# A graph layer on one core: TensorE waits for the end of its own rank products and of its own second filter layer

## The chip, the cores and the metric

The kernel runs on one NeuronCore of a Trainium2 chip. The engines named here are TensorE (PE, matmuls; its weight loads are listed apart as PEld), VectorE (DVE), ScalarE (ACT), GpSimd (POOL) and SyncE (SP, which issues DMAs). Each runs its own stream of instructions in order, and they meet only through semaphores. The metric is the device time of one execution in microseconds (us), the median of several runs; smaller is better.

## The reference, cut to what matters

A continuous-filter graph layer over 12,500 nodes with 128 features and 400,000 edges, sorted by `dst`:

```python
h = relu(layernorm(x)) @ W_in2f.T                    # 12500 x 128
Wij = smu(edge_attr @ W_f1.T + b_f1) @ W_f2.T + b_f2 # 400000 x 128, "two filter layers"
Wij = Wij * edge_weight[:, None]
x_ij = h[dst] * Wij
agg = segment_sum(x_ij, src)                         # sum of the edges of each node
out = x + smu(agg @ W_o1.T + b_o1) @ W_o2.T + b_o2
```

`smu(x)` is a smooth activation made here of a Gelu and a linear part. The edges come sorted by `dst`, but are summed by `src`, so the kernel has to sort the messages itself.

## The kernel before, in words

**Units.** The edges (padded) are cut into 784 units of 512 edges (4 tiles of 128). Each engine runs its own version of the function `step(st)` once for each beat, a beat being one unit; `st.at(k)`, `st.has(k)`, `st.items(k)` speak of the unit that lies k beats back, so each step works on several units at once, as a software pipeline. TensorE's step does, in this order:

- `filter1(n)` (L1202): first filter layer, into PSUM bank `p_z`. ScalarE takes the Gelu (`gelu`, L707), VectorE adds the linear part (`act`, L979).
- `bucket_sum(it)` (L1256, `p_seg`): for messages sorted in an earlier round, products of rows `seg` with one-hot matrices `seg_hot`. VectorE builds the one-hots (L1029) and adds the result to `agg` (L1042).
- `turn(n-2)` (L1213): transposes the product `hg` of unit n-2 into `p_m`, from where ScalarE writes the weighted messages `msg` (L723). It waits for VectorE's product (`s_prod`).
- `rank(n-1)` (L1228, L1244): eight small products into `p_pos` that count, for each edge, how many edges of its bucket came before it. The last one raises `s_rank`; VectorE's `places` (L1003) waits for that and works out the row of each edge, `row_numbers` (L1014).
- `targets(n-1)` (L1222): gathers `h[dst]` as a product with a window of rows (`win`), into `p_h`; ScalarE copies it to `hg` (L717).
- `filter2(n-1)` (L1207): second filter layer into `p_w`, raises `s_w`; VectorE multiplies it into `hg` (L995), which is what the next beat's `turn` waits for.

**GpSimd.** For each unit it waits for the row numbers, the messages and for `filter2` of two units later (`s_w`), and then issues four indirect DMAs, one for each tile, that scatter the messages into `sorted_rows` in DRAM (L588):

```python
wait_for(pool, s_idx, n, 1, 1)
wait_for(pool, s_msg, n, 1, 1)
wait_for(pool, s_w, n, 1, 3)
for k in range(tiles):
    pool.indirect_dma_start(out=sorted_rows[:, :], ...)
```

Messages, row numbers and one-hots have rings of four buffers (`RING`), so VectorE and ScalarE wait for the scatter of four units ago.

**Rounds.** The units form ten rounds of 112, 112, 112, 112, 80, 80, 56, 40, 40 and 40 units. The messages of a round fall into 112 buckets. Those of round r are summed (`bucket_sum`) during the beats of round r+1, eight beats late, spread evenly; round 9 is summed behind the last unit. A bucket takes 5, 5, 5, 5, 4, 4, 3, 2, 2, 2 tiles in rounds 0 to 9; of those with 4 and 3 tiles two buckets go together in one item, of those with 2 tiles four do. Each tile costs TensorE two matmul instructions. Parts of rounds 0 to 3 are hardware loops of four beats, all else is straight code.

The order of each engine's work is the order in which `step` is written. Nothing else schedules it. `wait_for(eng, sem, at, times, plus)` makes an engine wait until a semaphore holds the unit's number plus an offset.

Of the kernel before, what the change touches and what calls it, by code (L numbers as in the profile page):

```python
# [77 lines left out]
def wait_for(eng, sem, at, times=1, plus=0):  # L78
    v = at.value(times, plus)
    if at.i is None and v <= 0:  # L80
        return
    eng.wait_ge(sem, v)


def build(nc, n_nodes, n_edges, n_real, F, R, t):
# [47 lines left out]
    with ctx:  # L133
# [6 lines left out]
        def sem(name):  # L140
            return ctx.enter_context(nc.semaphore(name))
# [68 lines left out]
        with ExitStack() as ahead_only:  # L210
# [67 lines left out]
        s_z, s_gelu, s_smu, s_w, s_pick, s_ph, s_hg, s_prod, s_turn, s_msg, s_key = (  # L278
            sem(n) for n in ("s_z", "s_gelu", "s_smu", "s_w", "s_pick", "s_ph", "s_hg", "s_prod", "s_turn", "s_msg", "s_key"))
        s_hot, s_rank, s_place, s_idx, s_total, s_count = (  # L280
            sem(n) for n in ("s_hot", "s_rank", "s_place", "s_idx", "s_total", "s_count"))
# [34 lines left out]
        def h_at(st, lag):  # L316

            at = st.c - H_FROM - lag
            if st.i is not None or st.rnd > 0 or at < 0 or at % 2:
                return None  # L320
            g = H_AHEAD + at // 2
            return g if g < n_h else None
# [850 lines left out]
        def _(pe):  # L1173
            pe.wait_ge(s_pool, 4)

            def transpose_nodes(g):
                pe.wait_ge(s_hn, g + 1)
                if g >= 1:
                    pe.wait_ge(s_hTs, g)
                for k in range(H_TILES):  # L1180
                    last = pe.transpose(p_seg[0][:, k * LANES:(k + 1) * LANES], hn[:, g % 2, k, :], ident[:, :])
                last.then_inc(s_hT, 1)

            def first_layer(g):
                pe.wait_ge(s_hTs, g + 1)
                if g >= 1:
                    pe.wait_ge(s_hr, g)
                for k in range(H_TILES):
                    last = pe.matmul(h_bank(g)[:, k, :], hT[:, g % 2, k, :], w_in[:, :], start=True, stop=True)
                last.then_inc(s_hm, 1)  # L1190
# [7 lines left out]
            def filter1(n, p, q, v):  # L1198
                if v == 0:
                    wait_for(pe, s_attr[q], p.over(2), 16, 16)  # L1200
                wait_for(pe, s_smu, n)
                pe.matmul(p_z[:, :], w_f1[:, :], attr[:, q, v * UNIT:(v + 1) * UNIT], start=True, stop=True).then_inc(s_z, 1)  # L1202

            def filter2(n, v):
                wait_for(pe, s_smu, n, 1, 1)
                wait_for(pe, s_prod, n)
                pe.matmul(p_w[:, :, :].rearrange("f k e -> f (k e)"), w_f2[:, :], act1[:, v, :], start=True, stop=True).then_inc(s_w, 1)  # L1207

            def turn(n, v):
                wait_for(pe, s_prod, n, 1, 1)  # L1210
                wait_for(pe, s_msg, n)
                for k in range(TILES_U):
                    last = pe.transpose(p_m[:, k, :], hg[:, v, k, :], ident[:, :])  # L1213
                last.then_inc(s_turn, 1)

            def targets(n, p, q, v):
                if v == 0:
                    wait_for(pe, s_win[q], p.over(2), 16, 16)
                wait_for(pe, s_pick, n, 1, 1)
                wait_for(pe, s_hg, n)  # L1220
                for part in range(PARTS):
                    last = pe.matmul(p_h[:, :, :].rearrange("f k e -> f (k e)"), win[:, q, part * F:(part + 1) * F], pick[:, v, :],  # L1222
                                     start=(part == 0), stop=(part == PARTS - 1))
                last.then_inc(s_ph, 1)

            def counted(slot, rnd):
                for k in range(TILES_U):
                    last = pe.matmul(p_pos[:, 0:BUCKETS], not_before[:, :], onehot[:, slot, k, :], start=False, stop=False,  # L1228
                                     skip_group_check=True)
                return last  # L1230

            def rank(n, slot, rnd, opens):
                wait_for(pe, s_hot, n, 1, 1)
                wait_for(pe, s_place, n)
                if opens:
                    if rnd > 0:
                        counted((slot - 1) % RING, rnd - 1).then_inc(s_total, 1)
                        pe.wait_ge(s_count, rnd)
                    pe.matmul(p_pos[:, 0:BUCKETS], step_rows[:, :], seeds[:, rnd % BUFS, :], start=True, stop=False,
                              skip_group_check=True)  # L1240
                else:
                    counted((slot - 1) % RING, rnd)
                for k in range(TILES_U):
                    last = pe.matmul(p_pos[:, 0:BUCKETS], before[:, :], onehot[:, slot, k, :], start=False, stop=False,  # L1244
                                     skip_group_check=True)
                last.then_inc(s_rank, 1)

            def bucket_sum(it):
                wait_for(pe, s_segld[it.slot], it.x.over(SEGS), 16, 16)
                wait_for(pe, s_seghot, it.x, 1, 1)  # L1250
                if it.opens:
                    wait_for(pe, s_agg, it.n, 1, -1)
                for l in range(it.some):
                    out = p_seg[it.bank][:, it.col + l * NODE_P:it.col + (l + 1) * NODE_P]
                    for k in range(it.tiles):
                        last = pe.matmul(out, seg[:, it.slot, l * it.tiles + k, 0:F], seg_hot[:, it.slot, l * it.tiles + k, :],  # L1256
                                         start=(k == 0), stop=(k == it.tiles - 1))
                last.then_inc(s_seg, 1)

            def hidden(g, turn):  # L1260
                b, n = g % 2, turn * n_groups + g
                if turn == 0:
                    pe.wait_ge(s_agg, first_sum[rounds - 1] + g + 1)
                if n > 1:
                    pe.wait_ge(s_oe, n - 1)
                pe.matmul(p_u[b][:, :, :].rearrange("p a n -> p (a n)")[:, 0:GROUP], w_o1[:, :],
                          agg[:, g * NODE_G:(g + 1) * NODE_G, :], start=True, stop=True).then_inc(s_u, 1)
# [11 lines left out]
            def step(st):  # L1279
                if st.rnd == 0 and st.i is None and st.c == 1:  # L1280
                    pe.wait_ge(s_scaled, 1)
                    filter2(st.at(1), st.v(1))
                    pe.wait_ge(s_pool2, 2)
                    pe.wait_ge(s_seeds, 1)
                    rank(st.at(1), st.ring(1), st.rnd_of(1), st.opens(1))
                    targets(st.at(1), st.pair(1), st.q(1), st.v(1))
                    filter1(st.at(), st.pair(), st.q(), st.v())
                    transpose_nodes(1)
                    return
                if st.rnd == rounds - 1 and st.c == 0:  # L1290
                    pe.wait_ge(s_ld, 16 * N_LD)
                    pe.wait_ge(s_scaled_out, 1)
                if st.has():
                    filter1(st.at(), st.pair(), st.q(), st.v())
                for it in st.items(1):
                    bucket_sum(it)
                if st.has(2):
                    turn(st.at(2), st.v(2))
                if st.has(1):
                    rank(st.at(1), st.ring(1), st.rnd_of(1), st.opens(1))  # L1300
                    targets(st.at(1), st.pair(1), st.q(1), st.v(1))
                    filter2(st.at(1), st.v(1))
                if st.rnd == 0 and st.i is None and st.c == 2:
                    first_layer(1)
                if h_at(st, 1) is not None:
                    transpose_nodes(h_at(st, 1))
                if h_at(st, 3) is not None:
                    first_layer(h_at(st, 3))
                if st.i is None and st.rnd == rounds and st.c == 1:
                    pe.wait_ge(s_place, n_units)  # L1310
                    counted((n_units - 1) % RING, rounds - 1).then_inc(s_total, 1)
                if st.group(2) is not None:
                    hidden(st.group(2), 0)
                if st.group(4) is not None:
                    last_layer(st.group(4), 0)

            beats(pe, step)

            def everywhere():
# [84 lines left out]
```

## Time and profile before

| | |
|---|---|
| median of 3 runs | 4146.94 us (4142.5 to 4153.49) |
| the profiled execution, first to last instruction | 5246.4 us; no other time is reported for it |
| its mean granted TensorE clock | 0.902 of full speed |
| busy in it: PE, DVE, ACT, POOL | 4105.5, 3459.8, 2190.0, 3044.9 us |
| TensorE idle ahead of `turn` (L1213) in it | 905.9 us |

The profiled execution took 1,099 us longer than the median of the runs without a profile. So its sums of idle time can't be read as those of an ordinary run; durations of single instructions and the distance between two that follow each other without a wait can. The ends of TensorE's matmuls are modelled, and consecutive ones overlap in the records; the distance between two starts tells what one costs in a stream.

### The profile page before, as it was taken

The page shows a single profiled execution, that of the slowest core. Times are in us where ns is not written, and L with a number is a line of the kernel's source. Part 1 is how long each engine was busy: PE and PEld are TensorE (multiplying, and loading weights), DVE is VectorE, ACT ScalarE, POOL GpSimd, SP SyncE. Part 2 cuts the span into 40 slices and gives each one's busy share as a digit, 9 for nine tenths or more (in the row PEclk, how much of TensorE's full clock was granted, in tenths as well). Part 3 has the DMA queues.
Part 4 walks back from the last instruction along what each step waited for, and adds up shares of the span by engine and source line. Part 5 has one row for each costly group of instructions (what it writes and reads, how often), then busy time and mean ns, then how long its engine had stood idle before and what let it go on. Part 6 is the DMA issues. An engine that isn't in the chain of part 4 may idle for free.

```text
span 5246.4 us, 97364 instructions
## 1 busy us (share of the span) xinstructions
PE 4105.5 (78%) x23774; PEld 2777.5 (53%) x23774; DVE 3459.8 (66%) x11848; ACT 2190.0 (42%) x7302; POOL 3044.9 (58%) x3173
## 2 busy tenths in 40 slices
PE   6677667777777777777777778788888888887888
PEld 3344335555555555555555555555555666655557
DVE  6666556666666666666666666666666777766677
ACT  4566444444443344444443434434443443334333
POOL 4666655555555555555555555655555555555553
PEclk8888889988988989989889899998888999998999
DMA  6455445554444444444444445554444555554446
GB/s 181 122 147 147 126 118 144 147 144 146 146 133 125 125 124 125 131 127 125 127 126 121 134 145 148 148 153 132 132 133 136 158 157 152 159 160 136 139 137 206
DMA packets 459545, 737.14 MB, mean 141 GB/s; under 512 B 87168, under 2 KB 255466, under 8 KB 459104
## 3 DMA queue, kind: packets, MB, share of 16 engines
q1 hardware_dynamic: 291606, 461.44, 33.5%
q0 software_dynamic: 100000, 206.60, 11.7%
q10 hardware_dynamic: 67626, 65.48, 3.8%
q8 instruction: 129, 2.11, 0.2%
q14 instruction: 184, 1.51, 0.1%
HBM read 465.36 MB, written 267.82 MB: 140 GB/s over the span
## 4 chain that ended last, share of the span: by engine, by line
PE 36%; another core or an unknown queue 25%; DVE 16%; issue 14%; ACT 7%; ACTq 1%; DMA 1%; DVEq 1%; SPq 0%; POOL 0%
PE p_w L1207 7%; PE p_h L1222 7%; PE p_seg L1256 6%; PE p_m L1213 6%; PE p_z L1202 5%; DVE product L1003 4%; DVE hg L995 4%; ACT msg L723 3%; PE p_pos L1244 2%; DVE onehot L988 2%; PE p_pos L1228 2%; DVE act L979 2%; ACT hg L717 2%; DVE pick L983 1%
## 5 line engine op out<-in xcount | busy, mean ns | idle before, releaser
L588 POOL DMA_INDIRECT sorted_rows<-msg,row_idx x3125 | 3004.5, 961 | 2122.6 <-issue 904.5
L1003 DVE CUSTOM_DVE_ANT_0 product<-onehot,p_pos,start_at 128x112 bf16<-128x112 bf16 x3136 | 849.2, 326 | 1096.3 <-remote 1012.3
L723 ACT ACTIVATE msg<-p_m,weight 128x128 f32<-128x128 f32 x3136 | 893.5, 369 | 1439.1 <-remote 786.2
L1256 PEld LDWEIGHTS p_seg<-seg_hot,seg 128*128 128x128 f32 x8288 | 1066.4, 196 | 464.5 <-issue 461.8
L1213 PE MATMUL p_m<-ident,hg 128*128 128x128 f32 x3136 | 561.2, 307 | 905.9 <-DVE hg L995 649.7
L1256 PE MATMUL p_seg<-seg_hot,seg 128*128 128x112 f32 x8288 | 1085.6, 279 | 117.3 <-issue 107.8
L1213 PEld LDWEIGHTS p_m<-ident,hg 128*128 128x128 f32 x3136 | 384.5, 155 | 1102.0 <-DVE hg L995 675.3
L1207 PE MATMUL p_w<-act,w_f 128*128 128x512 f32 x1568 | 932.0, 679 | 10.4 <-issue 5.7
L1202 PE MATMUL p_z<-attr,w_f 128*128 128x512 f32 x1568 | 853.8, 626 | 56.3 <-issue 24.3
L995 DVE SCALAR_TENSOR_TENSOR hg<-p_w,bias_w,hg 128x512 f32<-128x512 f32 x784 | 588.0, 750 | 464.9 <-remote 155.4
L717 ACT COPY hg<-p_h 128x512 f32<-128x512 f32 x784 | 461.9, 589 | 878.4 <-remote 592.3
L1222 PE MATMUL p_h<-pick,win 128*128 128x512 bf16 x2352 | 767.9, 442 | 7.2 <-issue 5.1
L707 ACT ACTIVATE gelu<-p_z 128x512 f32<-128x512 f32 x784 | 468.5, 598 | 579.5 <-PE p_z L1202 324.7
L979 DVE SCALAR_TENSOR_TENSOR act<-p_z,gelu 128x512 f32<-128x512 f32 x784 | 537.1, 685 | 138.8 <-issue 93.9
L1202 PEld LDWEIGHTS p_z<-attr,w_f 128*128 128x128 f32 x1568 | 325.4, 212 | 510.9 <-issue 465.5
L1029 DVE SCALAR_TENSOR_TENSOR seg_hot<-seg,p_iota 128x560 f32<-128x560 f32 (+2 forms) x700 | 582.0, 837 | 11.9 <-DMA seg<-sorted_rows 7.3
L988 DVE TENSOR_TENSOR onehot<-p_iota,node_l 128x448 bf16<-128x448 f32 x784 | 481.7, 614 | 0.0
L1207 PEld LDWEIGHTS p_w<-act,w_f 128*128 128x128 f32 x1568 | 355.1, 227 | 170.6 <-issue 67.7
L1244 PE MATMUL p_pos<-onehot,before 128*128 128x112 bf16 x3136 | 320.1, 232 | 0.0
L1228 PE MATMUL p_pos<-onehot,not_before 128*128 128x112 bf16 x3136 | 316.1, 230 | 0.0
L983 DVE TENSOR_SCALAR pick<-ends,win_row 128x512 bf16<-128x512 uint16 x784 | 289.4, 369 | 0.0
L1222 PEld LDWEIGHTS p_h<-pick,win 128*128 128x128 bf16 x2352 | 218.9, 110 | 129.0 <-issue 56.4
(114 smaller groups left out, 2157.8 us busy)
## 6 DMA issues: line engine op xcount, KB each, us to landing
seg<-sorted_rows SPq DMA_DIRECT2D x448, 322.5 KB
seg<-sorted_rows SPq DMA_DIRECT2D x196, 516.0 KB
ends<-ends SPq DMA_DIRECT2D x392, 256.0 KB
sorted_rows<-msg,row_idx POOLq DMA_INDIRECT x3125
sorted_rows<-zero_rows ACTq DMA_DIRECT2D x336, 129.0 KB
win<-h SPq DMA_DIRECT2D x392, 96.0 KB
attr<-in_attrT SPq DMA_DIRECT2D x392, 80.0 KB
seg<-sorted_rows SPq DMA_DIRECT2D x56, 387.0 KB
```

Source lines behind the costliest of these rows:

```text
L588: pool.indirect_dma_start(out=sorted_rows[:, :], out_offset=bass.IndirectOffsetOnAxis(ap=row_idx[:, slot, k:k + 1], axis=0), in_=msg[:, sl ...
L723: last = act.activation(msg[:, slot, k, 0:F], p_m[:, k, :], ACT.Copy, scale=weight[:, bass.ds(n.value(TILES_U, k), 1)])
L979: dve.scalar_tensor_tensor(act1[:, v, :], p_z[:, :], SMU_L, gelu[:, v, :], ALU.mult, ALU.add).then_inc(s_smu, 1)
L988: dve.tensor_tensor(onehot[:, slot, :, :], p_iota[:, 0:BUCKETS].unsqueeze(1).to_broadcast([LANES, TILES_U, BUCKETS]), node_l[:, bass.ds(n. ...
L995: dve.scalar_tensor_tensor(hg[:, v, :, :], p_w[:, :, :], bias_w[:, :], hg[:, v, :, :], ALU.add, ALU.mult).then_inc(s_prod, 1)
L1003: last = dve.tensor_tensor_reduce(out=product[:, k, :], in0=onehot[:, slot, k, :], in1=p_pos[:, 0:BUCKETS], scale=1.0, scalar=start_at[:, ...
L1029: dve.scalar_tensor_tensor(seg_hot[:, it.slot, 0:n, :], seg[:, it.slot, 0:n, F:F + 1].to_broadcast([LANES, n, NODE_P]), -float(LANES * (it ...
L1202: pe.matmul(p_z[:, :], w_f1[:, :], attr[:, q, v * UNIT:(v + 1) * UNIT], start=True, stop=True).then_inc(s_z, 1)
L1207: pe.matmul(p_w[:, :, :].rearrange("f k e -> f (k e)"), w_f2[:, :], act1[:, v, :], start=True, stop=True).then_inc(s_w, 1)
L1213: last = pe.transpose(p_m[:, k, :], hg[:, v, k, :], ident[:, :])
L1222: last = pe.matmul(p_h[:, :, :].rearrange("f k e -> f (k e)"), win[:, q, part * F:(part + 1) * F], pick[:, v, :], start=(part == 0), stop= ...
L1256: last = pe.matmul(out, seg[:, it.slot, l * it.tiles + k, 0:F], seg_hot[:, it.slot, l * it.tiles + k, :], start=(k == 0), stop=(k == it.ti ...
```

## The change

TensorE's step gets two waits. The first stands between `rank` and `targets` and asks for the `s_rank` that its own last rank product has just been told to raise. The second stands behind `filter2` and asks for the `s_w` that this same layer raises. Nothing is removed or moved.

```diff
                 if st.has(1):
                     rank(st.at(1), st.ring(1), st.rnd_of(1), st.opens(1))
+                    wait_for(pe, s_rank, st.at(1), 1, 1)
                     targets(st.at(1), st.pair(1), st.q(1), st.v(1))
                     filter2(st.at(1), st.v(1))
+                    wait_for(pe, s_w, st.at(1), 1, 1)
```

The very first beat with such work is written out apart and has no new wait; 783 of the 784 units get both.

Where the waits land is to be seen in the order of TensorE's instructions, with the semaphores that each one waits for. First a beat in the middle of the loop body in round 1. Before, from the rank products to the bucket sum of the next beat:

```order
L1228 MATMUL p_pos<-onehot,not_before 128x112 [waits s_place,s_hot]
L1228 MATMUL p_pos<-onehot,not_before 128x112 x3
L1244 MATMUL p_pos<-onehot,before 128x112 x4
L1222 MATMUL p_h<-pick,win 128x512 [waits s_hg,s_pick]
L1222 MATMUL p_h<-pick,win 128x512 x2
L1207 MATMUL p_w<-act,w_f 128x512 [waits s_prod,s_smu]
L1202 MATMUL p_z<-attr,w_f 128x512 [waits s_smu]
```

The same beat of the changed kernel:

```order
L1228 MATMUL p_pos<-onehot,not_before 128x112 [waits s_place,s_hot]
L1228 MATMUL p_pos<-onehot,not_before 128x112 x3
L1244 MATMUL p_pos<-onehot,before 128x112 x4
L1222 MATMUL p_h<-pick,win 128x512 [waits s_hg,s_pick,s_rank]
L1222 MATMUL p_h<-pick,win 128x512 x2
L1207 MATMUL p_w<-act,w_f 128x512 [waits s_prod,s_smu]
L1202 MATMUL p_z<-attr,w_f 128x512 [waits s_smu,s_w]
```

The first target product now waits for the rank products, and the next beat's first filter layer (`p_z`) for the second filter layer (`p_w`). No row has changed its place.

At the end of a loop body the row behind `filter2` is no matmul. Before, TensorE's rows around the loop's counter (L401) in a straight piece ahead of the loop's next part:

```order
L1222 MATMUL p_h<-pick,win 128x512 x2
L1207 MATMUL p_w<-act,w_f 128x512 [waits s_prod,s_smu]
L401 REGISTER_ALU
L401 COMPARE_AND_BRANCH
L1202 MATMUL p_z<-attr,w_f 128x512 [waits s_smu,s_attr0]
```

And of the changed kernel:

```order
L1222 MATMUL p_h<-pick,win 128x512 x2
L1207 MATMUL p_w<-act,w_f 128x512 [waits s_prod,s_smu]
L401 REGISTER_ALU [waits s_w]
L401 COMPARE_AND_BRANCH
L1202 MATMUL p_z<-attr,w_f 128x512 [waits s_smu,s_attr0]
```

Here the second wait holds the counting and the branch themselves, once in four units of a loop.

## Rows read from the trace of the kernel before

**Rows 1.** The page's first line: the span.

```profile
span 5246.4 us, 97364 instructions
```

**Rows 2.** Waits by engine and line: total us, times, longest us.

```profile
DVE product L1003 <- remote: 1012.3, 310, 6.3
...
PE p_m L1213 <- DVE hg L995: 649.7, 302, 7.0
```

**Rows 3.** Timeline, 2000 to 2030 us: start, duration, engine, line, count, idle before.

```profile
2006.61 0.36 PE L1244 MATMUL p_pos<-onehot,before 128*128 128x112 bf16 x4
...
2013.07 0.33 DVE L1003 CUSTOM_DVE_ANT_0 product<-onehot,p_pos,start_at 128x112 bf16<-128x112 bf16 x1 [3.06 <-remote]
```

**Rows 4.** Timeline of POOL: the first scatter and the last two.

```profile
39.03 1.12 POOL L588 DMA_INDIRECT sorted_rows<-msg,row_idx  x1 [33.06 <-issue]
...
5130.91 0.95 POOL L588 DMA_INDIRECT sorted_rows<-msg,row_idx  x1 [0.30 <-issue]
5132.17 0.96 POOL L588 DMA_INDIRECT sorted_rows<-msg,row_idx  x1 [0.30 <-issue]
```

**Rows 5.** Groups by line and form: the scatters, and VectorE's one-hots for the sums.

```profile
L588 POOL DMA_INDIRECT sorted_rows<-msg,row_idx x3125 | 3004.5, 961 | 2122.6 <-issue 904.5 <-remote 706.2 <-PE p_w L1207 362.4
...
L1029 DVE SCALAR_TENSOR_TENSOR seg_hot<-seg,p_iota 128x560 f32<-128x560 f32 x448 | 324.7, 731 | 3.9 <-DMA ends<-ends 3.9
...
L1029 DVE SCALAR_TENSOR_TENSOR seg_hot<-seg,p_iota 128x896 f32<-128x896 f32 x196 | 211.3, 1078 | 7.4 <-DMA seg<-sorted_rows 7.3
...
L1029 DVE SCALAR_TENSOR_TENSOR seg_hot<-seg,p_iota 128x672 f32<-128x672 f32 x56 | 46.0, 845 | 0.6 <-DMA ends<-ends 0.6
```

**Rows 6.** Timeline of PE: one whole beat in round 2 without stops.

```profile
2001.60 0.66 PE L1213 MATMUL p_m<-ident,hg 128*128 128x128 f32 x4 [1.49 <-DVE hg L995]
2002.09 0.36 PE L1228 MATMUL p_pos<-onehot,not_before 128*128 128x112 bf16 x4
2002.29 0.36 PE L1244 MATMUL p_pos<-onehot,before 128*128 128x112 bf16 x4
2002.48 0.81 PE L1222 MATMUL p_h<-pick,win 128*128 128x512 bf16 x3
2003.13 1.02 PE L1207 MATMUL p_w<-act,w_f 128*128 128x512 f32 x2
2003.99 1.02 PE L1202 MATMUL p_z<-attr,w_f 128*128 128x512 f32 x2
2004.85 1.26 PE L1256 MATMUL p_seg<-seg_hot,seg 128*128 128x112 f32 x10
2005.95 0.63 PE L1213 MATMUL p_m<-ident,hg 128*128 128x128 f32 x4
2006.41 0.36 PE L1228 MATMUL p_pos<-onehot,not_before 128*128 128x112 bf16 x4
```

**Rows 7.** Timeline of PE: a sum of 16 matmuls and what follows it.

```profile
3600.11 1.93 PE L1256 MATMUL p_seg<-seg_hot,seg 128*128 128x112 f32 x16
3601.88 0.60 PE L1213 MATMUL p_m<-ident,hg 128*128 128x128 f32 x4
```

**Rows 8.** Source view of L1244, 2100 to 2137 us: shortest, median and longest ns.

```profile
L1244 PE MATMUL p_pos<-onehot,before x24: 212/213/213, 2100.6 to 2132.3; 128*128 128x112 bf16 x24
```

**Rows 9.** Timeline, 2000 to 2030 us: what PE waited for, and who waited for PE.

```profile
2000.79 0.75 DVE L995 SCALAR_TENSOR_TENSOR hg<-p_w,bias_w,hg 128x512 f32<-128x512 f32 x1 [1.66 <-remote]
...
2002.39 1.14 ACT L723 ACTIVATE msg<-p_m,weight 128x128 f32<-128x128 f32 x4 [0.94 <-PE p_m L1213]
```

**Rows 10.** Timeline of PE behind a long stop.

```profile
2017.02 1.49 PE L1222 MATMUL p_h<-pick,win 128*128 128x512 bf16 x3
2018.30 1.53 PE L1207 MATMUL p_w<-act,w_f 128*128 128x512 f32 x2
```

**Rows 11.** Windows: busy PE, PEld, DVE, ACT, POOL with counts, PE clock, DMA share.

```profile
500.00:1000.00 500.00, 348.57 (x1803) 210.78 (x1802) 299.13 (x1076) 213.40 (x705) 298.35 (x309) 0.88 0.48 133
...
3000.00:3500.00 500.00, 407.71 (x2540) 288.28 (x2539) 343.93 (x1169) 201.06 (x692) 294.41 (x307) 0.94 0.51 149
```

## The prediction

> **What bounds the kernel now.** I read the page first. Its span is 5246.4 us [rows 1], 1,099 us above the median of the runs, 4146.94 us. So before anything is summed it has to be said what the profiled execution has that the others lack.
>
> The list of waits says it. VectorE's `product` waited 310 times for something unnamed, 1012.3 us in all, and TensorE's `turn` 649.7 us for the product that VectorE then made late [rows 2]. The timeline shows one such case: the rank products were over at 2006.61 + 0.36 = 2006.97, and VectorE, which waits for nothing else there, started at 2013.07 [rows 3], 6.1 us later. News of TensorE's finished work arrives late in this execution, and 1012 us of it is about the excess of 1,099 us. I take that lag for a thing of the recorded execution; that it is none of the others' follows only from the size of the excess.
>
> What then bounds an ordinary run? GpSimd's timeline: two scatters without a wait between them start 1.26 us apart (0.96 busy, 0.30 issue), the first at 39.03 us, the last ends at 5133.1 us [rows 4]. There are 3125 [rows 5]. Back to back they take 3125 x 1.26 = 3938 us; with 39 us ahead of them and 5246.4 - 5133.1 = 113 us behind, 4090 us. The median is 57 us above. So an ordinary run is one chain of scatters on GpSimd, nearly without holes: **5.04 us a unit**.
>
> TensorE's beat comes from the timeline where it doesn't stop [rows 6], always from start to start: `turn` 0.46 (0.49 behind a wait), rank 0.20 + 0.19, `targets` 0.65, `filter2` 0.86, `filter1` 0.86, ten sum matmuls 1.10. That is 3.25 us without sums plus 0.11 us for each sum matmul (sixteen take 1.77 us [rows 7]). How many there are in a unit follows from the rounds; the one-hots' rows confirm the total: 448 items of 5 tiles, 196 of 8, 56 of 6 [rows 5], 4144 tiles or 8288 matmuls.
>
> - 120 units ahead of the first sums: 3.25 us a beat
> - 336 units (rounds 1 to 3), 10 matmuls each: 4.35
> - 80 (round 4), 14: 4.79
> - 80 (round 5) and 40 (round 8), 11.2: 4.48
> - 56 (round 6), 16: 5.01
> - 40 (round 7), 16.8: 5.10
> - 32 (round 9), 14: 4.79
>
> TensorE has 0.7 us to spare in most beats at full clock, and nothing in rounds 6 and 7.
>
> **The change part by part.** Nothing is removed or moved; 783 units get two waits. Each wait holds TensorE until its own last matmul is out and the semaphore is back.
>
> What one costs isn't in this trace, since TensorE never waits there for itself. It is made of three parts. First the drain: a lone rank product takes 213 ns [rows 8] though in the stream they start 50 ns apart, and the row of four ends at 2002.65 while `targets` has started at 2002.48; 0.17 us. For `filter2` the row ends at 2004.15, the next starts at 2003.99; 0.16 us [rows 6]. Second the handover: the nearest row is TensorE resuming 0.06 us after VectorE's end (2001.54 to 2001.60); the other way, ScalarE starts 0.13 us after TensorE's modelled end (2002.26 to 2002.39) [rows 6, 9]. Third the weight load, which no longer hides under the matmul before it: the resumed `turn` takes 0.49 us and the unstopped one 0.46 [rows 6], 0.03 us. I take 0.17 + 0.06 + 0.03, about 0.25 us a wait, **0.5 us a unit**, since the waiter is TensorE as in the 0.06 row. Bounds: the drain alone, 0.33 us a unit; with the long handover, 0.68. Neither end can be a gain by itself, as a wait only holds. Far beyond these ends lies the 6.1 us of rows 3: it would make the profiled execution much longer, but it isn't what the ordinary runs show.
>
> The Trainium skill, "Advanced Engine Details and Errata", section Network/Comms, has a sequencer read a semaphore's value in 50 to 100 ns. By that figure as the handover, without the weight load, the sum below would be 59 to 80 us (an estimate from that page), and no row here shows the reading by itself.
>
> What is queued behind the waits: behind the first `targets` and `filter2`, which ScalarE's `hg`, VectorE's product and, through `s_w`, GpSimd wait for; behind the second `filter1`, the sums and the next `turn`. Does that lateness reach VectorE first? Counting from the start of `turn`, `filter2` is over at 2.39 + 0.16 us, with the first wait 2.8. VectorE is busy 3459.8 us in 784 units, 4.4 us a unit; all of that but the product itself, 0.75 us [rows 9], comes ahead of its need for `filter2`, about 3.6 us. So the first wait is hidden from VectorE by 0.8 us of its own work; if that cover were gone, 0.25 us a unit or 196 us would show. What counts is TensorE's beat against GpSimd's 5.04 us.
>
> With 0.5 us more a beat:
>
> - first 120 units 3.75, rounds 1 to 3 4.85, rounds 5 and 8 4.98: all still below 5.04, no cost. The idle time ahead of `turn` pays for it.
> - round 4: 5.29, 0.25 over, x 80 = 20 us
> - round 6: 5.51, 0.47 x 56 = 26 us
> - round 7: 5.60 instead of 5.10, 0.50 x 40 = 20 us
> - round 9: 5.29, 0.25 x 32 = 8 us
>
> Sum 74 us: **4147 + 74 = 4221 us**, 1.8% slower. With 0.33 us a unit the same list gives 6 + 17 + 13 + 3 = 39 us (4186). With 0.68, round 4 gives 34, rounds 5 and 8 now 0.12 x 120 = 14, then 36, 27 and 14: 125 us (4272). The loop's branch, now held by the second wait too, comes once in four units of rounds 0 to 3, where 0.19 us of a beat are still free; I cost it at nothing. If it took over 0.8 us, it would show.
>
> These sums are made on the median, with durations of the profiled execution; by its own span the forecast says nothing, since its lag may shrink or grow with the waits.
>
> **The rivals.**
>
> *The idle time swallows it.* TensorE has 906 us of idle time ahead of `turn` in the profile, 650 of them a wait for VectorE [rows 2]. If a self-wait costs 0.1 us, or if the dense rounds have slack that my averages miss (the row of four scatter buffers carries a slow beat over a fast one), only rounds 6 and 7 show it: at 0.2 us a unit 10 + 8 = 18 us, at 0.1 us a unit 7 us. Against it: the drain alone is 0.33 us. Time 4147 to 4159, say 4152. Chance 0.20.
>
> *The clock falls.* Behind the long stop TensorE ran `targets` in 1.28 us from start to start instead of 0.65 [rows 6, 10]: exactly half, 1.2 GHz instead of 2.4 GHz. The granted clock was 0.88 in an early window with 349 us of busy TensorE and 0.94 in one with 408 [rows 11]. If the small holes made 5% of TensorE's work run at the lower level, each beat would be 0.05 x 4.35 = 0.22 us longer, 0.72 in all, and the list gives 150 us (4297); at 10%, 0.93 in all, 288 us (4435), as rounds 1 to 3 then pass 5.04 too. Against it: the holes take the place of a longer one ahead of `turn`, so TensorE is idle no more than before. The Trainium skill, "TensorE: Matmul & The Clock Gate", section "A second HAM failure mode: psum-queue depth-cycling", reports just this, frequent micro-idles between groups of matmuls making the clock swing; the long stops of this trace show the fall, its short ones don't. Chance 0.10.
>
> *Faster.* If part of the lag of rows 3 is there in ordinary runs too, because TensorE races ahead of its own news, a TensorE held back would hand `s_rank` and `s_w` over sooner and GpSimd would have fewer holes. It can win no more than the 57 us above the bare chain: 4090 us. It decides once it wins back more than the waits cost, 39 us or more by the sums above; half of 57 isn't enough. Chance 0.07.
>
> **How the numbers follow.** The main case (4186 to 4272, 4221 the likeliest) has 0.63, the rivals 0.20, 0.10 and 0.07. A difference under 0.3% (12 us) can't be told from none. Slower: 0.63 + 0.10 = 0.73; same: 0.20; faster: 0.07. The range goes from 4142, which takes in the idle-time case, to 4300, which takes in the main case and the mild end of the clock case; what is left out is the faster case and most of the clock case, 0.07 + 0.07, and a few parts in a hundred between.
>
> **What would show it.** In the profile after: `targets` starting some 0.3 us after the last rank product's start instead of 0.05 us, and `filter1` likewise 0.25 us later behind `filter2`; TensorE's idle time ahead of L1222 and L1202 now tenths of a us in each of 783 units, that ahead of `turn` smaller; scatters still 1.26 us apart. Wrong would make it: an own wait that takes far more than 0.3 us; a mean clock below 0.88; beats of rounds 1 to 3 above 5.04 us; or scatters that are less than 1.26 us apart in ordinary runs, as then rounds 1 to 3 pay too, up to 0.5 x 336 = 168 us.

## The result and the profile after

The changed kernel takes 4244.39 us (median of 4 runs, 4236.25 to 4246.63), the kernel before 4148.44 us beside it: a ratio of 1.0228, 95% interval 1.0215 to 1.0241. That is 96 us or 2.3% slower, where 74 us or 1.8% (4221 us) was forecast. The last comparison below (e9 to e12) stands apart, because on its chip the unchanged kernel took 5249 us, as in the recorded execution shown above, instead of 4149 us.

The page of the changed kernel, with the lines that answer to [rows 1] and the table of before:

```profile
span 4233.8 us, 98063 instructions
...
PE 3901.1 (92%) x23774; PEld 2470.1 (58%) x23774; DVE 3461.2 (82%) x11848; ACT 2246.9 (53%) x7302; POOL 3043.5 (72%) x3173
```

The run that this is the record of took 4236.25 us, 2.5 us more than its span. The three others took 4244 to 4247 us, so the record is of the fastest run, 8 us below the median; its mean granted clock is 0.992. It has no lag, and idle times too can be read here as those of an ordinary run.

TensorE's timeline in round 5, the answer to [rows 6]: one beat with both waits and a sum of 16 matmuls (the last row opens the next beat).

```profile
3001.61 0.60 PE L1213 MATMUL p_m<-ident,hg 128*128 128x128 f32 x4
3002.05 0.36 PE L1228 MATMUL p_pos<-onehot,not_before 128*128 128x112 bf16 x4
3002.25 0.36 PE L1244 MATMUL p_pos<-onehot,before 128*128 128x112 bf16 x4
3002.67 0.82 PE L1222 MATMUL p_h<-pick,win 128*128 128x512 bf16 x3
3003.32 1.02 PE L1207 MATMUL p_w<-act,w_f 128*128 128x512 f32 x2
3004.41 1.12 PE L1202 MATMUL p_z<-attr,w_f 128*128 128x512 f32 x2
3005.37 1.94 PE L1256 MATMUL p_seg<-seg_hot,seg 128*128 128x112 f32 x16
3007.14 0.60 PE L1213 MATMUL p_m<-ident,hg 128*128 128x128 f32 x4
```

Read the starts. From the last rank row to the targets it is now 0.42 us instead of 0.19: the first wait costs 0.23 us. From `filter2` to `filter1` it is 1.09 us instead of 0.86, again 0.23. And `filter1` itself now takes 0.96 us to the next start instead of 0.86: 0.10 us that the prediction had no term for. The beat is 5.53 us; without waits the prediction's rows give 3.25 + 16 x 0.11 = 5.01. The 3.25 has `turn` at its 0.49 us behind a wait. Where nothing stops, `turn` takes 0.44 us, and most such beats without the new waits are 4.96 or 4.97 us long (the record of e3 below, round 6), so the pair of waits adds 0.56.

At the end of a loop body the second wait costs more. The same view at about 1500 us, in round 2:

```profile
1503.47 1.02 PE L1207 MATMUL p_w<-act,w_f 128*128 128x512 f32 x2
1505.09 1.12 PE L1202 MATMUL p_z<-attr,w_f 128*128 128x512 f32 x2 [0.60 <-PE p_w L1207]
1506.05 1.26 PE L1256 MATMUL p_seg<-seg_hot,seg 128*128 128x112 f32 x10
1507.15 0.60 PE L1213 MATMUL p_m<-ident,hg 128*128 128x128 f32 x4
```

1.62 us from start to start instead of 0.86, once in four beats.

The waits of the changed kernel (total us, times, longest us), beside which stand those of [rows 2]:

```profile
PEld p_z L1202 <- PE p_w L1207: 379.1, 420, 1.7
...
PEld p_h L1222 <- PE p_pos L1244: 164.2, 748, 0.3
...
PE p_m L1213 <- DVE hg L995: 121.4, 94, 3.4
```

TensorE now waits for itself some 750 times at the targets, 0.22 us each. The 379.1 us of the first row are no price: a stop of PEld is counted from the end of its last weight load, and that load hides under the matmul ahead (at 3004.40 it counts 0.89 us where the start of the matmul moved by 0.23), so most of it is time in which `filter2` still ran. For VectorE's product TensorE waits 121 us. In the record of e5 below, whose time is that of before, that is 295.6 us, and its idle time ahead of `turn` from all causes is 433.9 us, against 123.7 us here: the new waits took the place of part of the old one.

GpSimd over 500 us of rounds 1 and 2, and over 500 us that take in the end of round 5, round 6 and the start of round 7, the answer to [rows 11] (columns as there):

```profile
1000.00:1500.00 500.00, 469.15 (x2872) 296.98 (x2871) 413.68 (x1454) 272.95 (x892) 379.40 (x396) 1.00 0.62 172
...
3000.00:3500.00 500.00, 480.78 (x3044) 317.04 (x3043) 415.24 (x1360) 249.31 (x830) 353.53 (x370) 1.00 0.62 176
```

396 scatters in 500 us are one in 1.263 us: GpSimd has no hole here, and it has none in the record of e5 either (395). From 3000 us on there are 370, where e5's record has 389, and TensorE is busy 480.8 of 500 us. That is the kink that the prediction was built on: GpSimd is the bound in rounds 1 to 3, TensorE in the dense ones.

### The profile page after: what moved, and what is told of

It is laid out like the page before. It is cut to its first block, busy times and chain, and to the rows that moved or that the text cites. A ratio compares the mean times of both kernels' runs of the same rounds, so it can differ in the third digit from the quotient of the medians.

```text
span 4233.8 us, 98063 instructions
## 1 busy us (share of the span) xinstructions
PE 3901.1 (92%) x23774; PEld 2470.1 (58%) x23774; DVE 3461.2 (82%) x11848; ACT 2246.9 (53%) x7302; POOL 3043.5 (72%) x3173
## 4 chain that ended last, share of the span: by engine, by line
PE 64%; POOL 12%; issue 11%; DMA 6%; DVE 4%; ACT 2%; ACTq 1%; SPq 0%; POOLq 0%; DVEq 0%
PE p_seg L1256 16%; PE p_z L1202 13%; POOL sorted_rows L588 12%; PE p_w L1207 11%; PE p_h L1222 11%; PE p_m L1213 6%; DMA sorted_rows<-msg,row_idx 5%; PE p_pos L1244 3%; PE p_pos L1228 2%; DVE hg L995 1%; DVE product L1003 1%; DVE seg_hot L1029 1%; ACT msg L723 1%; PE p_seg L1189 1%; DVE act L979 1%
## 5 line engine op out<-in xcount | busy, mean ns | idle before, releaser
L1256 PEld LDWEIGHTS p_seg<-seg_hot,seg 128*128 128x128 f32 x8288 | 1029.0, 192 | 307.4 <-issue 304.6
L1256 PE MATMUL p_seg<-seg_hot,seg 128*128 128x112 f32 x8288 | 1024.8, 275 | 8.3 <-issue 8.3
L1207 PE MATMUL p_w<-act,w_f 128*128 128x512 f32 x1568 | 811.7, 600 | 4.2 <-DVE act L979 4.2
L1222 PE MATMUL p_h<-pick,win 128*128 128x512 bf16 x2352 | 652.5, 387 | 50.1 <-DMA win<-h 1.7
L1202 PEld LDWEIGHTS p_z<-attr,w_f 128*128 128x128 f32 x1568 | 234.5, 189 | 747.6 <-PE p_w L1207 379.1
L1213 PE MATMUL p_m<-ident,hg 128*128 128x128 f32 x3136 | 479.4, 276 | 123.7 <-DVE hg L995 121.4
L1207 PEld LDWEIGHTS p_w<-act,w_f 128*128 128x128 f32 x1568 | 302.5, 193 | 120.9 <-issue 9.2
L1014 DVE TENSOR_TENSOR row_idx<-place,place_max 128x4 int32<-128x4 f32 x784 | 126.0, 161 | 266.3 <-DMA sorted_rows<-msg,row_idx 257.7
L1222 PEld LDWEIGHTS p_h<-pick,win 128*128 128x128 bf16 x2352 | 166.6, 98 | 269.7 <-PE p_pos L1244 164.2
L1244 PE MATMUL p_pos<-onehot,before 128*128 128x112 bf16 x3136 | 284.2, 214 | 0.0
```

## The experiments

Each ratio is to the kernel before, run beside it. A unit is 1/784 of the work.

**e1, the first wait only.**

```diff
                     rank(st.at(1), st.ring(1), st.rnd_of(1), st.opens(1))
+                    wait_for(pe, s_rank, st.at(1), 1, 1)
                     targets(st.at(1), st.pair(1), st.q(1), st.v(1))
```

> Only the wait behind the rank products. My theory: a beat of TensorE costs time only above the 5.04 us that GpSimd's four scatters take, and this wait is 0.23 us (the distance from the last row of rank products to the target products grew from 0.19 to 0.42 us in the profile of the changed kernel). Round 6 is then 5.24 us a beat (0.20 x 56 = 11 us), round 7 5.33 instead of 5.10 (0.23 x 40 = 9 us), all others below 5.04: 20 us slower, about 4168 us, far less than half of the 96 us. Rival, every wait costs the same wherever it stands (0.06 us each of 1566): half of 96, 48 us slower, 4196 us.

Measured: 4187.45 us against 4149.48, ratio 1.009 (1.0073 to 1.0107), 38 us. Nearer to the rival's 48 than to my 20.

**e2, the second wait only.**

```diff
                     filter2(st.at(1), st.v(1))
+                    wait_for(pe, s_w, st.at(1), 1, 1)
```

> Only the wait behind the second filter layer. My theory: it costs 0.33 us a beat in straight code (0.23 more ahead of the first filter layer, 0.10 more in it), so rounds 4, 6, 7 and 9 pay 6 + 17 + 13 + 3 = 39 us: about 4187 us; in the loops of rounds 1 to 3 it costs 0.46 on the mean, which 4.35 us a beat still hides. The two waits alone then give 20 + 39 = 59 us, less than the 96 us together. Rival, every wait costs the same wherever it stands: 48 us each, and the two alone add up to the 96 us.

Measured: 4190.09 us, ratio 1.0099 (1.0082 to 1.0116), 41 us, the number that my theory had, but in part by luck. Round by round (the lengths come below) its record has 14 us in round 0, where the theory had nothing, and 6 us in round 6, where it had 17; rounds 4 and 7 cost 5 and 16 us against 6 and 13. The two waits alone make 79 us; together they make 96. So they don't simply add up, though less sharply than 59 against 96.

**e3 and e4, both waits, but only in the beats of rounds 0 to 3, or only in those of rounds 4 to 9.**

```diff
+                    if st.rnd < 4:
+                        wait_for(pe, s_rank, st.at(1), 1, 1)
                     targets(st.at(1), st.pair(1), st.q(1), st.v(1))
                     filter2(st.at(1), st.v(1))
+                    if st.rnd < 4:
+                        wait_for(pe, s_w, st.at(1), 1, 1)
```

(e4 has `st.rnd >= 4` in both places.)

> Both waits, but only in the beats of rounds 0 to 3 (448 of 784 units). My theory: GpSimd's chain hides them there, at most the loops' beats (4.35 + 0.56 + 0.13 = 5.04 us) touch the bound: 0 to 18 us slower, 4148 to 4166 us. Rival, the same cost in every unit: 448/784 of 96 us, 55 us slower.

> Both waits, but only in the beats of rounds 4 to 9 (336 of 784 units). My theory: nearly the whole loss is made here: with 0.56 us a beat, round 4 pays 0.31 x 80 = 25 us, round 6 0.53 x 56 = 30, round 7 0.56 x 40 = 22, round 9 0.31 x 32 = 10, rounds 5 and 8 nothing: 87 us slower, 4235 us. Rival, the same cost in every unit: 336/784 of 96 us, 41 us slower.

Measured: e3 4170.1 us, 1.0049 (1.003 to 1.0068), 21 us for 448 units; e4 4232.59 us, 1.0208 (1.0191 to 1.0225), 83 us for 336 units. The rival's 55 and 41 us are both out. e3 is above the 4148 to 4166 us that I had allowed, and not for the reason given there: the loops' beats cost nothing (rounds 1 to 3 of its record take 1701.3 us, those of e4 without waits 1705.1), while its round 0 took 606.7 us against 582.9. The pair of waits costs 0.05 us a unit over rounds 0 to 3 and 0.25 us over rounds 4 to 9.

These two also give a baseline round by round: what e4 does in rounds 0 to 3, and e3 in rounds 4 to 9, is the kernel before. Each round opens with one product of `seeds` (L1239), and the source view gives the start of the first and the last in a stretch. The changed kernel:

```profile
L1239 PE MATMUL p_pos<-seeds,step_rows x2: 224/263/302, 21.5 to 622.3; 128*128 128x112 bf16 x2
L1239 PE MATMUL p_pos<-seeds,step_rows x2: 222/223/224, 2323.1 to 2749.3; 128*128 128x112 bf16 x2
L1239 PE MATMUL p_pos<-seeds,step_rows x2: 223/248/273, 3162.9 to 3471.8; 128*128 128x112 bf16 x2
L1239 PE MATMUL p_pos<-seeds,step_rows x2: 222/223/224, 3700.8 to 3910.3; 128*128 128x112 bf16 x2
```

e4 for the early rounds:

```profile
L1239 PE MATMUL p_pos<-seeds,step_rows x2: 223/262/301, 21.2 to 604.1; 128*128 128x112 bf16 x2
L1239 PE MATMUL p_pos<-seeds,step_rows x2: 223/223/223, 2309.2 to 2736.7; 128*128 128x112 bf16 x2
```

e3 for the late ones, and its span:

```profile
span 4169.4 us, 97350 instructions
...
L1239 PE MATMUL p_pos<-seeds,step_rows x2: 223/224/224, 2329.5 to 2736.1; 128*128 128x112 bf16 x2
L1239 PE MATMUL p_pos<-seeds,step_rows x2: 223/224/225, 3146.2 to 3439.4; 128*128 128x112 bf16 x2
L1239 PE MATMUL p_pos<-seeds,step_rows x2: 223/224/224, 3646.6 to 3851.8; 128*128 128x112 bf16 x2
```

The lengths are the differences of these starts:

| beats of | without waits, us | with, us | more | forecast |
|---|---|---|---|---|
| round 0 (112) | 582.9 | 600.8 | +18 | 0 |
| rounds 1 to 3 (336) | 1705.1 | 1700.8 | -4 | 0 |
| round 4 (80) | 406.6 | 426.2 | +20 | 20 |
| round 5 (80) | 410.1 | 413.6 | +4 | 0 |
| round 6 (56) | 293.2 | 308.9 | +16 | 26 |
| round 7 (40) | 207.2 | 229.0 | +22 | 20 |
| round 8 (40) | 205.2 | 209.5 | +4 | 0 |
| round 9 and what follows | 317.6 | 323.5 | +6 | 8 |

The left column with 21.2 us ahead of it sums to 4149 us, within the spans of the kernel before beside these runs (4142 to 4151 us): the pieces fit. But each length is from one record. That of e5 below, whose time is also that of before, has 592.4 us for round 0 and lies within 4 us of the left column everywhere else. So a round's cost is known to some 4 us, and that of round 0 only as 8 to 18 us.

**Where round 0 lost its time.** GpSimd in windows of 60 us (busy with count, PE clock, DMA share, GB/s), the changed kernel first, then e4, which has no waits here:

```profile
240.00:300.00 60.00, 41.35 (x44) 0.97 0.63 172
300.00:360.00 60.00, 40.72 (x43) 0.94 0.62 168
360.00:420.00 60.00, 40.73 (x43) 0.94 0.61 162
```

```profile
240.00:300.00 60.00, 45.31 (x48) 0.97 0.69 182
300.00:360.00 60.00, 44.21 (x46) 1.00 0.66 182
360.00:420.00 60.00, 45.66 (x48) 1.00 0.72 190
```

130 scatters instead of 142: twelve times 1.26 us is 15 us. (e5's record has 136 in these windows.) In these beats TensorE, ScalarE and VectorE also make the node layer's rows (`transpose_nodes`, `first_layer`). I had counted the beats of round 0 as 3.25 us throughout and forgotten that work. That it is this work that takes up the slack is read from the place, not tried by a kernel of its own; e10 and e11 below show only that a longer GpSimd covers the waits here too.

**e5, the same two waits, each one group of matmuls later.**

```diff
                 if st.has():
                     filter1(st.at(), st.pair(), st.q(), st.v())
+                if st.has(2):
+                    wait_for(pe, s_w, st.at(2), 1, 1)
...
                     targets(st.at(1), st.pair(1), st.q(1), st.v(1))
+                    wait_for(pe, s_rank, st.at(1), 1, 1)
                     filter2(st.at(1), st.v(1))
```

> The same two semaphores are waited for, each one group of matmuls later: the rank products' behind the target products (0.65 us of other work in between), the second filter layer's behind the next beat's first filter layer (0.86 us in between). My theory: what costs is the array running dry, not the wait as an instruction; here the semaphore has long risen when TensorE asks, so the time is that of before, 4149 us, within 10 us. Rival, the wait itself costs (sequencer time, or its instructions): the 96 us of both waits, 4245 us.

Measured: 4151.88 us against 4153.08, ratio 0.9994 (0.9984 to 1.0003). As many waits, no cost, and that in the dense rounds as well, where nothing would hide one: rounds 4, 6 and 7 take 406.2, 290.8 and 207.0 us, against the 406.6, 293.2 and 207.2 of the table. So it isn't the instruction or the sequencer's work on it that costs, but TensorE standing still until its own last matmul is out and the semaphore is back. One group of other matmuls in between is enough. How the price divides into drain, handover and weight load this run doesn't tell.

**e6, a third wait of the same kind.**

```diff
                     turn(st.at(2), st.v(2))
+                    wait_for(pe, s_turn, st.at(2), 1, 1)
```

> A third wait of the same kind, for TensorE's own turned product right behind turn. It makes a beat 0.23 to 0.25 us longer again: 0.8 us in straight code, 0.9 to 1.0 in the loops. My theory: rounds 1 to 3 now stand above GpSimd's 5.04 us too, so this wait costs far more than the two before it together would suggest: 0.25 x 300 in the loops, 0.24 x 120 in rounds 5 and 8, 0.25 x 208 in rounds 4, 6, 7 and 9, about 75 + 29 + 52 = 156 us on top of the 96: about 4400 us. Rival, the same price for each wait: 48 us more, 4293 us.

Measured: 4385.76 us, ratio 1.0558 (1.054 to 1.0576): all three cost 233 us, so the third adds 137 us to the 96 of the first two. Expected were 156 us, by the rival 48. The openings in its record show that rounds 1 to 3 pay now:

```profile
L1239 PE MATMUL p_pos<-seeds,step_rows x2: 223/262/301, 21.2 to 631.2; 128*128 128x112 bf16 x2
L1239 PE MATMUL p_pos<-seeds,step_rows x2: 222/222/223, 2403.2 to 2848.0; 128*128 128x112 bf16 x2
```

2403.2 - 631.2 = 1772 us for 336 units, 5.27 us each, against 1705 us without waits and 1701 with two. With two waits the loops' beats stood at 5.05 us on the mean; the third wait is the one that lifts TensorE over GpSimd's 5.04 us.

**e7 and e8, the first filter layer done twice in each beat (the second overwrites the same values), without and with the waits.**

```diff
+                pe.matmul(p_z[:, :], w_f1[:, :], attr[:, q, v * UNIT:(v + 1) * UNIT], start=True, stop=True)
                 pe.matmul(p_z[:, :], w_f1[:, :], attr[:, q, v * UNIT:(v + 1) * UNIT], start=True, stop=True).then_inc(s_z, 1)
```

> The kernel before, with the first filter layer's matmul done twice in each beat (the second overwrites the same values), as the base for the next run: TensorE has 0.86 us more to do in each beat, so that it and not GpSimd is the bound wherever sums are made: 5.21 us in rounds 1 to 3. Sum of the beats with GpSimd's 5.04 us as a floor: about 4400 us. If TensorE had more to spare than I think, nearer to 4150 us.

> The same with both waits. My theory: without GpSimd's cover each wait shows in full in the 664 units with sums: 0.56 us x 364 in straight code and 0.75 x 300 in loops, about 430 us more than the run with the first filter layer done twice and no waits, against 96 us between the kernel pair as it was. Rival, the same price wherever it stands: 96 us more here as well.

Measured: e7 4358.21 us, 1.0488 (1.0471 to 1.0506); e8 4790.23 us, 1.1529 (1.1509 to 1.1548). e7 had been expected at about 4400 us and came 42 us lower: its rounds 1 to 3 take 5.15 us a unit, not 5.21. The same two waits cost 432 us here, against 430 expected and 96 us in the kernel pair. The openings of rounds 1 to 4, e7 first, show where:

```profile
L1240 PE MATMUL p_pos<-seeds,step_rows x4: 222/223/223, 628.7 to 2360.1; 128*128 128x112 bf16 x4
```

```profile
L1240 PE MATMUL p_pos<-seeds,step_rows x4: 222/223/223, 637.8 to 2612.8; 128*128 128x112 bf16 x4
```

The 336 units of rounds 1 to 3 take 1731.4 us without the waits and 1975.0 with them, 0.73 us more a unit; the same units with the same waits cost nothing in the pair. With no cover each wait shows in full. These two runs settle the kink, together with e3 and e4.

**e9 to e12.** These four ran on another chip, and there the unchanged kernel took 5248.71 us (7 runs, 5242.49 to 5265.73). Its ratios don't compare with those above.

> The kernel before, unchanged, recorded once more. Its first recorded execution took 5246 us against 4149 us of the others, with TensorE's semaphores seen up to 6 us late. The recorded executions of the kernels with one late pair of waits, and of the one with the first filter layer twice and no waits, agree with their unrecorded times within 0.1%. If the lag is a chance event of one recording, the span is now near 4150 us; if it comes with this program whenever it is recorded, near 5250 us again. In both cases the time without a record stays at 4149 us.

Measured for e9: 5250.84 us, the kernel before once more. The page's span and the first waits:

```profile
span 5249.0 us, 97364 instructions
...
DVE product L1003 <- remote: 1028.5, 327, 6.4
```

1028.5 us of the same unnamed wait as in [rows 2]. The seven other runs of this kernel on this chip took as long, and the 24 others on record took 4142 to 4161 us. So the lag is no accident of one record, and it doesn't come with the program alone; it came with this chip or this occasion.

e10 and e11 put a small fill behind each of GpSimd's scatters (and a wait for the fills of the unit before), without and with the two waits:

```diff
                     pool.indirect_dma_start(...).then_inc(s_scat[slot], 16)
+                    last = pool.memset(idle_rows[:, k, :], 0.0)
+                if tiles:
+                    last.then_inc(s_idle, 1)
```

> The kernel before, with a small fill of an unused tile behind each scatter on GpSimd (four a unit, of 128 x 128 elements), as the base for the next run. At about 0.2 us each, as for the fills of that size at the start of the program, a unit takes GpSimd 5.84 us instead of 5.04: about 4149 + 784 x 0.8 = 4780 us. Should the fills hide beside the scatters, it stays nearer to 4149 us.

> The same with both waits. My theory: TensorE's longest beat with waits, 5.7 us in round 7, is now below GpSimd's 5.84 us, so that the waits cost nothing anywhere: within 10 us of the run with the longer GpSimd and no waits. Rival, TensorE's waits cost by themselves: 96 us more.

Measured: e10 5021.51 us, ratio 0.9557 (0.9529 to 0.9584) to the kernel before on that chip; e11 5353.9 us, 1.0212 (1.015 to 1.0274), 332 us more than e10 where none were expected. As a whole that doesn't answer whether a longer GpSimd hides the waits, since with the lag an own wait can take far more than 0.23 us. By rounds it does for a part. The openings of rounds 4 to 7, e10 first:

```profile
L1246 PE MATMUL p_pos<-seeds,step_rows x4: 223/223/223, 2802.8 to 4162.6; 128*128 128x112 bf16 x4
```

```profile
L1246 PE MATMUL p_pos<-seeds,step_rows x4: 222/223/223, 3084.6 to 4442.1; 128*128 128x112 bf16 x4
```

Rounds 4 to 6 take 1359.8 us without the waits and 1357.5 with them, where the pair lost 39 us. Round 0 takes 699.8 and 699.2 us, rounds 8 and 9 the same to 1 us: in these 408 units the longer GpSimd hides both waits. The loss lies in rounds 1 to 3 (283 us) and 7 (37 us); the two records are 317 us apart, the medians 332. The lag falls just as unevenly. TensorE's stops at the targets for something unnamed, first in e11's rounds 1 to 3, then in its rounds 4 to 6:

```profile
PE p_h L1229 <- remote: 350.2, 131, 3.5
```

```profile
PE p_h L1229 <- remote: 31.6, 17, 2.5
```

And e10 by itself shows a unit of GpSimd in its timeline:

```profile
3004.33 0.97 POOL L592 DMA_INDIRECT sorted_rows<-msg,row_idx  x1 [0.93 <-POOL idle_rows L595]
...
3010.48 0.96 POOL L592 DMA_INDIRECT sorted_rows<-msg,row_idx  x1 [0.93 <-POOL idle_rows L595]
```

6.15 us, not the 5.84 expected: the wait for the fills holds each unit's first scatter 0.93 us. 784 such units are 4822 us of its 5021, and the 4149 us of the kernel before without lag, plus 784 x (6.15 - 5.04), make 5019. So in e10 GpSimd covers the lag almost whole. Its record has about half of it: VectorE's `product` waited 506.7 us in 309 times, against 1028.5 us in e9. The kernel is 227 us faster on that chip than the kernel before, though its GpSimd has 1.1 us more to do in each unit. Why the lag is smaller beside a longer GpSimd stays open.

e12 is the changed kernel with the second wait at the head of the next beat:

```diff
+                if st.has(2):
+                    wait_for(pe, s_w, st.at(2), 1, 1)
                 if st.has():
                     filter1(st.at(), st.pair(), st.q(), st.v())
...
                     filter2(st.at(1), st.v(1))
-                    wait_for(pe, s_w, st.at(1), 1, 1)
```

> Both waits, but the second stands at the head of the next beat, ahead of its first filter layer, instead of at the end of its own beat. Between the two places lie only the loop's counter and branch. The wait then no longer holds these: in the loops (328 units, one end in four) the distance from the second filter layer to the first falls from 1.62 to about 1.16 us. My theory: rounds 1 to 3 are hidden under GpSimd's 5.04 us either way, so the time stays within 8 us of 4244 us. Rival, the branch carries part of the loss: 0.46 x 82 = 38 us faster, 4206 us.

Measured: 6164.39 us, ratio 1.1767 (1.1709 to 1.1824) on that chip. Its timeline shows what the lag does to an own wait:

```profile
2005.55 0.36 PE L1244 MATMUL p_pos<-onehot,before 128*128 128x112 bf16 x4
...
2009.27 0.33 DVE L1003 CUSTOM_DVE_ANT_0 product<-onehot,p_pos,start_at 128x112 bf16<-128x112 bf16 x1 [3.14 <-remote]
...
2009.29 0.82 PE L1222 MATMUL p_h<-pick,win 128*128 128x512 bf16 x3 [3.38 <-remote]
```

The rank products were over at 2005.91; VectorE and TensorE both went on at 2009.27 to 2009.29, 3.4 us later. TensorE, which used to run on through such a lag, now stands still in it: 419 times at the targets in this record, 1322.2 us. It doesn't come with every wait: in the next beat `filter1` resumed after 0.23 us. What the branch in the loops costs in time can't be told from this run; without the lag it wasn't tried.

## Why the prediction was right, step by step

**GpSimd as the bound** was right: 396 scatters in 500 us in the changed kernel, rounds 1 to 3 at 1705 / 336 = 5.07 us a unit before, e7 and e8 with the cover taken away, and rounds 4 to 6 of e10 and e11 with more of it.

**The price of a wait** was forecast at 0.25 us each, 0.5 a unit, and came out at 0.23 each plus 0.10 in `filter1`, 0.56 a unit. The three parts that I had taken, drain, short handover and weight load, sum to 0.26 and 0.25; only their sum was measured, 0.23, not each by itself. The 0.10 is a term that was missing. The record places it in the first of the layer's two matmuls, 0.696 us long where the second has 0.592. Its weight load starts with it, at 3004.40; in e5's record the load starts 0.43 us ahead of its matmul (3002.53 against 3002.96). That this unhidden load is the 0.10 is read from there, not tried. e5 shows that the price isn't the wait as an instruction.

**The sum over the rounds** was 74 us; the records give 85, the medians 96 (the changed kernel's record is of its fastest run, 8 us under the median). Rounds 4, 7 and 9 came out within 2 us of the forecast, round 4 by two errors that cancel: the pair costs 0.56 us and not 0.5, but the beats already took 5.08 us without it, not 5.04. Two terms were mis-sized. "First 120 units 3.75 ... no cost" was wrong by 8 to 18 us: those beats carry the node layer too. And round 6 was to cost 26 us and cost 16. Its beat with waits was right (308.9 / 56 = 5.52 us, forecast 5.51); what the sum lacked is one long stop that the round already had. In e3's record, without waits there:

```profile
3430.77 1.11 PE L1213 MATMUL p_m<-ident,hg 128*128 128x128 f32 x4 [8.11 <-DVE hg L995]
```

That beat is 14.7 us long (14.6 in e5's record), while most others are 4.97. VectorE was late because it had waited 9.5 us for a scatter to land. With the waits the same beat takes 9.5 us, so that they cost some 5 us less there than in a round without such a stop. So it is partly luck that 74 is as near to 96 as it is: 10 us too many in round 6 stand against 8 to 18 missing in round 0. Rounds 5 and 8, with a mean of 5.04 us by the rows, cost 4 us each: their beats differ, 5.53 us with an item of 16 matmuls and mostly 3.75 without one, and one mean held against one floor doesn't show that.

**e1 came out at 38 us where I expected 20**, by the same omissions: its round 0 was 598.4 us long against e4's 582.9 (592.4 in e5's record), and round 8, where I had nothing, cost 5 us; round 6 cost 4 us instead of 11.

**The loops' branch** was costed at nothing unless it took over 0.8 us. It took 0.53 us more than the straight place; the beats there are 5.39 us once and 4.93 three times, 5.05 on the mean, and rounds 1 to 3 lost nothing.

**The rivals.** That idle time swallows it holds for rounds 1 to 3 and not elsewhere. The clock did not fall: the mean granted clock is 0.992, above the 0.98 of e5, whose time is that of before. The holes are short, and most of the stop ahead of `turn` went. The Trainium skill, "TensorE: Matmul & The Clock Gate", section "A second HAM failure mode: psum-queue depth-cycling", has frequent micro-idles between groups of matmuls make the clock swing. This trace doesn't show it: some 1,500 added holes of a quarter of a microsecond, and every stretch of 500 us from 500 to 4000 us at 0.99 or 1.00. The faster case, a TensorE held back handing its semaphores over sooner, isn't seen: e5, which holds it back at no cost, gains nothing.

**Wrong was the step on the lag**: "I take that lag for a thing of the recorded execution". e9 and the seven runs of the same kernel beside it all took 5242 to 5266 us, and the 24 others none over 4161. The forecast did not hang on it, since it was made on the median and from pieces without stops; but a reader of the sentence would expect it never to matter, and there it costs 1,100 us in every run.

## What to carry to other kernels

In this kernel a wait for TensorE's own last matmul cost about a quarter of a microsecond, and nothing if one group of other matmuls (0.65 or 0.86 us) stood between. What it does to the time is decided beat by beat: a pair of waits that was free under another engine's 5.04 us cost its full price in the dense stretch, and the third one cost more than the first two together. Sum over stretches, take each one's own bound from a clean record, and ask of each what else runs in it.

## What the runs showed of the hardware that I had not expected

- The same program took 4149 us on some occasions and 5249 us on another, each steady to 0.5%, with news of TensorE's finished rank products up to 6 us late and a mean clock of 0.905 instead of 0.98. It isn't news alone: ahead of its own sum matmuls TensorE stopped for nothing that the profile names 177 times, 107.8 us in all, in the record of before (106.3 us in e9's), against 8.3 us in that of the changed kernel. The kernels reacted very differently: e10 took 0.956 of the kernel before there, e12 1.177. What makes the lag isn't known.
- Behind an own wait the first filter layer, two matmuls with 512 columns in f32, takes 0.10 us longer by itself, all of it in the first of the two.
- With 1,566 added waits the mean granted clock was not lower but higher, 0.992 against the 0.98 of e5's record.
- At a loop's end a wait held the counter and the branch, and the next matmul came 0.53 us later than in straight code.
